# Joining the feed-forward, the second cross attention and the LoRA layer of a gated two-block transformer in one program of eight slots per tile

## The reference

```python
x = x + tanh(g_xattn[0]) * L0_xattn(layernorm(x), ctx, ctx, mask, wq, wk, wv, wo)   # 32 query heads, 8 kv heads, RoPE
x = x + tanh(g_ffn[0])   * L0_ffn(layernorm(x), Wg, Wu, Wd)
x = x + tanh(g_xattn[1]) * L1_xattn(layernorm(x), ctx, Wq, bq, Wk, bk, Wv, bv)
x = x + tanh(g_ffn[1])   * L1_ffn(layernorm(x), W_base, b_base, lora_A, lora_B, router_W, router_b, prior, active)

def L0_ffn(x):            # F = 1376; weights quantised to 4 bits per row, activations to 8 bits per token
    h = silu(quant_linear(x, Wg)) * quant_linear(x, Wu)
    return quant_linear(h, Wd)
def L1_xattn(x, init):    # per sequence: channels C = 64, "time" T = 512
    q, k = Wq @ init + bq, Wk @ init + bk
    return softmax(q.T @ k) @ (Wv @ x + bv)        # T x T weights for each of 16 sequences
def L1_ffn(x):            # four active experts of rank 8
    y = x @ W_base.T + b_base
    alpha = softmax(log(prior + EPS) + router(x))[active]
    return y + sum_e alpha_e * 2.0 * (x @ A_e.T) @ B_e.T
```

## Time and profile before

| | us |
|---|---|
| median of 3 runs (lowest, highest) | 946.81 (945.67, 949.27) |
| the profiled execution, its own time | 948.28 |
| its span, from first to last instruction | 946.3 |

### The profile page before, as it was taken

One profiled execution on the slowest core, in us unless ns is written; L12 is line 12 of the kernel. 1 busy time (PEld: TensorE's weight loads), 2 busy tenths in 40 slices (PEclk: granted clock), 3 DMA queues, 4 the chain that ended last, 5 costly groups with the idle time before them and its releaser, 6 DMA issues. The chain is left out here.

```text
span 946.3 us, 14460 instructions
## 1 busy us (share of the span) xinstructions
PE 856.0 (90%) x5009; PEld 652.6 (69%) x5009; DVE 594.7 (63%) x1291; ACT 485.4 (51%) x1059; POOL 489.1 (52%) x502
## 2 busy tenths in 40 slices
PE   4689999999999999999999999976995688888885
PEld 4567888888888787888888888753442466666664
DVE  3447667676676566665755555677983666666652
ACT  2444556555555454545445434336874666666541
POOL 1477556565575665656656755413454344444441
PEclk9799999999999999999999999988998899999998
DMA  8501221331331330421310405520000000000000
GB/s 239 141 19 56 92 81 35 114 94 34 118 92 29 98 99 11 119 68 29 115 43 18 24 1 204 131 89 1 1 0 1 1 1 12 11 11 11 11 12 23
DMA packets 66796, 54.14 MB, mean 57 GB/s; under 512 B 34560, under 2 KB 52192, under 8 KB 66352
## 3 DMA queue, kind: packets, MB, share of 16 engines
q1 hardware_dynamic: 66448, 53.36, 20.0%
q10 hardware_dynamic: 288, 0.00, 0.0%
HBM read 47.01 MB, written 6.34 MB: 56 GB/s over the span
## 5 line engine op out<-in xcount | busy, mean ns | idle before, releaser
L846 POOL TENSOR_TENSOR rope_swap<-rope_swap,trig 128x512 f32<-128x512 f32 x80 | 108.6, 1357 | 198.4 <-ACT rope_swap L562 197.2
L704 DVE TENSOR_TENSOR rope_cos<-bank,trig 128x512 f32<-128x512 f32 x80 | 55.3, 691 | 135.6 <-PE bank L79 135.6
L561 ACT COPY rope_swap<-bank 64x512 f32<-64x512 f32 x80 | 46.7, 584 | 166.8 <-DVE rope_cos L704 166.8
L1848 POOL TENSOR_TENSOR b_e<-b_e,b_inv 128x512 f32<-128x512 f32 x64 | 66.7, 1041 | 108.0 <-DVE b_inv L1637 108.0
L77 PE MATMUL bank<-xnT_hi,wq_hi 128*128 128x512 f32 x256 | 106.1, 414 | 4.8 <-issue 3.2
L453 PE MATMUL bank<-wo_hi,oT_hi 128*128 128x512 f32 x256 | 106.7, 417 | 1.1 <-ACT oT_hi L639 1.1
L79 PE MATMUL bank<-xnT_hi,wq_lo 128*128 128x512 f32 x256 | 101.5, 396 | 0.0
L78 PE MATMUL bank<-xnT_lo,wq_hi 128*128 128x512 f32 x256 | 101.3, 396 | 0.0
L454 PE MATMUL bank<-wo_lo,oT_hi 128*128 128x512 f32 x256 | 100.8, 394 | 0.0
L731 DVE SCALAR_TENSOR_TENSOR x_res<-bank,gate,x_res 128x512 f32<-128x512 f32 x128 | 88.6, 732 | 3.6 <-PE bank L458 3.6
L852 POOL TENSOR_TENSOR q_rope<-rope_cos,rope_swap 128x512 f32<-128x512 f32 x64 | 84.2, 1315 | 5.0
(11 more groups left out here) (215 smaller groups left out, 2058.9 us busy)
## 6 DMA issues: line engine op xcount, KB each, us to landing
wq_raw<-in_L_xattn_wq SPq DMA_DIRECT2D x16, 512.0 KB, 5.2
wo_raw<-in_L_xattn_wo SPq DMA_DIRECT2D x16, 512.0 KB, 5.5
w_T_dram<-w_out SPq DMA_DIRECT2D x28, 128.0 KB, 3.0
w_T<-w_T_dram SPq DMA_DIRECT2D x2, 1376.0 KB, 7.3
q_rope<-in_ctx SPq DMA_DIRECT2D x4, 512.0 KB, 5.9
wkv_raw<-in_L_xattn_wk SPq DMA_DIRECT2D x8, 256.0 KB, 3.1
wkv_raw<-in_L_xattn_wv SPq DMA_DIRECT2D x8, 256.0 KB, 3.6
x_res<-in_x SPq DMA_DIRECT2D x4, 512.0 KB, 10.0
```

Source lines behind the costliest of these rows:

```text
L704: dve.tensor_tensor(out=rope_cos[:, rp, :].rearrange("p (b s) -> p b s", s=S), in0=proj[pos % 2][:, :].rearrange("p (b s) -> p b s", s=S), ...
L846: pool.tensor_tensor(out=sw, in0=sw, in1=sin_b, op=ALU.mult).then_inc(s_rope, 1)
L1848: pool.tensor_tensor(out=e[n % 4][:, :], in0=e[n % 4][:, :], in1=inv_total[:, n:n + 1].to_broadcast([P, D]), op=ALU.mult).then_inc(s_w, 1)
```

## The change

The first attention stays, but its last three slots on VectorE also take the layer-norm statistics of the first six tiles, which `block1_weights` did before, and after the last slot come their aggregation and one power on GpSimd.

The three later programs become one, `tail_block`. It has 10 iterations of eight slots, all written out. In iteration `it` it works on four tiles: f = it (feed-forward), a = it - 1 (second attention, middle part), y = it - 2 (LoRA layer), nx = it + 1 (q and k of the next tile, and its activation scale). One block of weights runs per slot, m = 8 it + s - 4. The making of the weights is spread over slots 0 to 3 of iteration 0. Further:

- The PSUM banks are shared. `eT_ps` has one bank. `misc_ps` serves q, k, v, the transposes of x, x3 and the end of h. `gate_ps` serves gate, the transpose of h and down. `up_ps` serves up and the first half of the base product with the low-rank columns (292 columns); `y1_ps` the second half and LoRA.
- The weights of q and k stand side by side, so one product makes q and k of one sequence. ScalarE makes the high part of all 128 partitions in one instruction, VectorE the low part in one, and SP copies the halves into the stacked layout with five DMAs per sequence (64 x 512 float32, 128 KB each).
- Silu becomes Tanh: VectorE scales up by half the scale, GpSimd makes gate * up, and VectorE makes (tanh + 1) times that (`make_h`).
- The normalisations of all three layer norms go from VectorE to GpSimd.
- The result is made in three instructions of 256 columns instead of one of 512.

```diff
 def attention_block(...):            # VectorE, slot()
+                if last and jp == 1 and u > 0:
+                    for tl in range(2):
+                        dve.wait_ge(s_acc, 2 * U + tl + 1)
+                        dve.bn_stats(K.stats[:, 2 * u - 2 + tl, :], K.x[:, 2 * u - 2 + tl, :]).then_inc(s_x_stat, 1)
...
-def ffn_block(cx, K, W): ...
-def block1_weights(cx, K, W, R, ctx_dram): ...
-def block1(cx, K, W, out_dram): ...
+def tail_block(cx, K, W, W1, R, ctx_dram, out_dram):
+        def run_slots(slot):
+            for it in range(NT + 2):
+                for s in range(NS):
+                    slot(it, s, NS * it + s - 4, it, it - 1, it - 2, it + 1)
+        # TensorE
+            def gate_up(t, n):
+                if n == 0:
+                    pe.wait_ge(s_xT_sb, t + 1)
+                    after(pe, s_out, t)
+                    after(pe, s_res, t - 2)
...
+            def attend(t, tb):
+                pe.wait_ge(s_eT_sb, NB * t + 2 * tb + 2)
+                if tb == 0:
+                    pe.wait_ge(s_v, t + 1)
...
+            def z_T(t):
+                pe.wait_ge(s_z, 5 * t + 5)
...
+            def slot(it, s, m, f, a, y, nx):
+                if is_logit(m): logits(m)
+                if is_logit(m - 2): weights_T(m - 2)
+                if s == 0: gate_up(f, 0)
+                if s == 1: x3_T(y); gate_up(f, 1)
+                if s == 2: gate_up(f, 2); v_item(a)
+                if s in (3, 4, 5, 6): attend(a, s - 3)
+                if s == 3: base_low(y)
+                if s == 4: qk(nx, 0)
+                if s == 5: z_T(y); qk(nx, 1)
+                if s == 6: h_transpose(f); lora_base(y)
+                if s == 7: down(f); x_transpose(nx)
+        # VectorE (in iteration 0 the steps of the weights stand in slots 0 to 3 as well)
+            def slot(it, s, m, f, a, y, nx):
+                row_max(m)
+                if s == 0: output(a)
+                if s == 1: statistics(a)
+                reciprocal(m)
+                if s == 0: scale_gate_up(f, 0)
+                if s == 1: x3_lo(y); scale_gate_up(f, 1); make_h(f, 0)
+                if s == 2: scale_gate_up(f, 2); make_h(f, 1)
+                if s == 3: make_h(f, 2); add_v(a)
+                if s == 4: route(y); h_scales(f); lo_qk(nx, 0)
+                if s == 5: route_end(y); lo_qk(nx, 1)
+                if s == 6: zT_lo(y); front(nx)
+                if s == 7: finish(y); residual(a)
+        # ScalarE
+            def slot(it, s, m, f, a, y, nx):
+                if s == 7: hT_copy(f)
+                if s == 5: h_int(f)
+                copy_T(m - 2); exps(m)
+                if s == 0: tanh_half(f, 0)
+                if s == 1: x3_hi(y); tanh_half(f, 1)
+                if s == 2: tanh_half(f, 2)
+                if s == 4: route_exp(y); h_shifted(f); hi_qk(nx, 0)
+                if s == 5: hi_qk(nx, 1); zT_copy(y)
+                if s == 6: x_shifted(nx); x_int(nx)
+                if s == 7: xT_copy(nx)
+        # GpSimd
+            def slot(it, s, m, f, a, y, nx):
+                weigh(m - 1)
+                if s == 0: add(a)
+                if s in (1, 2, 3): product(f, s - 1)
+                if s == 1: std(a); normalise(a)
+                if s == 5: add_bias(y); front(nx)
+                if s == 7: x3_std(a); x3_normalise(a)
+        # SyncE
+            def duplicate(t, par):
+                after(sp, s_r, NB * (t - 1))
+                sp.wait_ge(s_qk_lo, 2 * t + par + 1)
+                for dst, src in ((q_stack[i][par][lower, :], qk_hi[par][lower, :]), ...):   # five
+                    sp.dma_start(f32(dst), f32(src)).then_inc(s_dup[i][par], 16)
+            # slot 5: duplicate(nx, 0); slot 6: duplicate(nx, 1), the next context tile; slot 7: store(y)
```

More of the change, by code:

```diff
@@ new lines, in tail_block @@
+        e = [sb(f"b_e{i}", [P, D]) for i in range(4)]
+        eT = sb2("b_eT", [P, DC, D])
+        bT = e[0]
+        x3_stats, x3_mv, x3_ve, x3_rstd = sb("b_x3_stats", [P, 6]), sb("b_x3_mv", [P, 2]), sb("b_x3_ve", [P, 1]), sb("b_x3_rstd", [P, 1])
+        pad = sb("b_pad", [P, 1])
+        logit, neg_lmax, lsum, linv = sb("b_logit", [P, E_ACT]), sb("b_neg_lmax", [P, 1]), sb("b_lsum", [P, 1]), sb("b_linv", [P, 1])
+        alpha = sb("b_alpha", [P, E_ACT])
+        z = sb("b_z", [P, ZREP, E_ACT, RANK])
@@ new lines, in tail_block, with ok, is_logit, after @@
+        s_y, s_res = sem("s_b_y"), sem("s_b_res")
+        s_part = sem("s_b_part")
+        s_store = [sem(f"s_b_store{i}") for i in range(2)]
+        def run_slots(slot):
+            for it in range(NT + 2):
+                for s in range(NS):
+                    slot(it, s, NS * it + s - 4, it, it - 1, it - 2, it + 1)
+        def ok(t):
+            return 0 <= t < NT
+        def is_logit(m):
+            return 0 <= m < NB * NT
+        def after(eng, s, value):
+            if value > 0:
+                eng.wait_ge(s, value)
@@ new lines, in _ @@
+            front(0)
+            selection()
+            def slot(it, s, m, f, a, y, nx):
+                if is_logit(m):
+                    row_max(m)
+                if s == 0:
+                    if ok(a):
+                        output(a)
+                if s == 1 and ok(a):
+                    statistics(a)
+                if is_logit(m):
+                    reciprocal(m)
+                if s == 0:
+                    if it == 0:
+                        base_lo(0)
+                        lo_qk(0, 0)
+                    if ok(f):
+                        scale_gate_up(f, 0)
+                if s == 1:
+                    if it == 0:
+                        base_lo(1)
+                        lo_qk(0, 1)
+                    if ok(y):
+                        x3_lo(y)
+                    if ok(f):
+                        scale_gate_up(f, 1)
+                        make_h(f, 0)
+                if s == 2:
+                    if it == 0:
+                        base_lo(2)
+                        base_lo(3)
+                    if ok(f):
+                        scale_gate_up(f, 2)
+                        make_h(f, 1)
+                if s == 3:
+                    if it == 0:
+                        low_lo()
+                        low_b_lo()
+                        rest_of_weights()
+                        late_statistics()
+                    if ok(f):
+                        make_h(f, 2)
+                    if ok(a):
+                        add_v(a)
+                if s == 4:
+                    if ok(y):
+                        route(y)
+                    if ok(f):
+                        h_scales(f)
+                    if ok(nx):
+                        lo_qk(nx, 0)
+                if s == 5:
+                    if ok(y):
+                        route_end(y)
+                    if ok(nx):
+                        lo_qk(nx, 1)
+                if s == 6:
+                    if ok(y):
+                        zT_lo(y)
+                    if ok(nx):
+                        front(nx)
+                if s == 7:
+                    if ok(y):
+                        finish(y)
+                    if ok(a):
+                        residual(a)
```

1513 lines of the change are left out of this document (694 added, 819 removed).

## The result

The changed kernel takes 1041.95 us (median of 4 runs, 1041.03 to 1042.75) against 946.28 us (945.67 to 949.27) for the kernel before in the same session: a ratio of 1.1004, 95% interval 1.0978 to 1.1029. It is slower, as forecast, and inside the range of 965 to 1048, but 29 us above the forecast of 1013 and above the 998 to 1028 that the forecast gave as its own range. The profiled execution has a span of 1040.4 us at a mean granted clock of 0.924 (before: 946.3 and 0.968).

A forecast was written before the change was run, and what follows sets the result against it. The second attention was taken as paced by VectorE's own list, waits included. List and exponential waits 29.0 + stalls 11.3 + clock 2.4 + make_h 1.0 gave P = 43.7; 706.3 + 7 P = 1012.2, forecast 1013 us, range 965 to 1048.

The forecast's parts named there:

- slots 3 and 4, b_v to the logits: VectorE's maximum in slot 4 waits for attend, twelve products and logits queued behind b_v: 3.5 us.
- clock: After TensorE's two long waits per iteration, 3 us each at the lower clock: 2.4 us, bounds 0 and 5.
- neighbouring iterations 42 to 45 us apart: Sign in the new trace: the same VectorE step in neighbouring iterations stands 42 to 45 us apart.
- the upper end, three full lengths: Three make_h per tile, each blocked by GpSimd for up to its full length: 3 us; 1.0 was taken.
- the price put on that (1.5 per tile): Normalisation on GpSimd, bounded by 0.53 and 2.1 us: costs 0 at the 1.04 taken, 1.5 per tile at the upper end.
- 706.3 + 7 P: Whole span from the tail's start, edge iterations and P, the period of one iteration: 1012.2 us at P = 43.7.
- iteration 8: 20; iteration 9: 17.2: The last two tail iterations: 20 us, then 17.2 us for the LoRA chain alone at half clock and the store.
- The break-even: The iteration period at which the changed kernel equals the kernel before: P = 34.3 us.
- Rival B: Run-ahead leaves VectorE only its list and six unfilled exponentials: P = 29.0, 905 us; chance 0.12.
- A: Rival: TensorE keeps its full clock and make_h is not blocked: P = 40.3, 989 us; chance 0.22.
- D: Rival: the DMA copies are late, more than 6 us each: P some 52, 1071 us; chance 0.03.
- C: Rival: make_h blocking at its upper end, GpSimd normalisations at 2.1 us, low clock after each wait: 1045 us; chance 0.15.

The follow-up runs named there:

- e_fill: Changed kernel plus unread TensorE products (12 before the first attend, 18 before the transpose of z) during its waits: 1022.32 us.
- e_norm: Changed kernel with a tile's three normalisations moved back from GpSimd to VectorE: 1045.13 us.
- e_b2: e_b1 with VectorE steps already due placed between maximum and reciprocal in slots 2, 4, 6 and 7: 939.01 us, ratio 0.9898.
- e_b1: Changed kernel with the reorderings of e_addv, e_low, e_qk, h_int behind the exponential, lora_base in slot 7, residual before finish: 971.02 us.
- e_b3: e_b2 with b_v before slot 2's make_h, last make_h and route_end filling exponential waits, slot 5's high q and k before h_int: 913.76 us.
- e_late: Changed kernel with a tile's ten DMA copies issued only after down of the tile before: 1041.20 us.
- e_addv: Changed kernel with VectorE's b_v step in slot 3 moved between the maximum and the reciprocal: 1022.72 us.
- e_low: Changed kernel with TensorE's twelve 292-column products moved in slot 3 ahead of the first attend: 1023.02 us.
- e_rec: Changed kernel with VectorE steps already due placed between maximum and reciprocal in slots 2, 4, 6 and 7: 1002.90 us.
- e_qk: Changed kernel with slot 4's high half of q and k before h_shifted, and slot 5's second q and k before the transpose of z: 1029.19 us.
- e_hint: Changed kernel with ScalarE's h_int (slot 5) and copies of transposed h (slot 7) moved behind the slot's exponential: 1044.65 us.

## Why the prediction was right, and where its size was off

The forecast rested on VectorE's list per iteration and on stalls named one by one. Against the timeline of one iteration (809.77 to 856.42, 46.65 us):

| step | predicted | measured | at full clock (e_fill) |
|---|---|---|---|
| VectorE's list, with make_h blocked | 25.2 | 25.43 | 25.43 |
| waits for exponentials, slots 2 to 7 | 6.1 | 6.48 | 6.49 |
| slot 0, gate behind output | 1.1 | 1.10 | 1.10 |
| slots 3 and 4, b_v to the logits | 3.5 | 5.84 | 3.51 |
| slot 4, first lo_qk | 2.1 | 1.85 | 1.85 |
| slot 5, second lo_qk | 2.1 | 3.00 | 2.00 |
| slots 6 and 7, logits behind lora_base | 1.5 | 1.34 | 1.33 |
| waits for GpSimd (x_res, the product) | none | 1.00 | 1.00 |
| clock | 2.4 | in the rows above, 3.3 | 0 |

(Overlap was put at -0.3; gaps of VectorE too short for the view are 0.6.)

- The mechanism was right in every place it named, and e_fill gives each row back to within 0.4 us once the clock is held up. But the sign named for it, neighbouring iterations 42 to 45 us apart, was missed: they stand 45.9 to 47.2 apart. The walk through the order, with durations from the trace of before, was enough to find them.
- The clock was undersized: "2.4 us" was 3.3 by the two stalls (2.9 by P in e_fill). The prediction took 3 us at the lower level after each wait, and it was six after the first (0.50 from 872 to 878): attend, products and logits all ran in it.
- `make_h` was sized rightly: 24 of them take 21.6 us; at 0.68, 0.68 and 0.52 unblocked they would be 15.0, so 0.8 us per tile against the 1.0 taken. The instance at 868.28 takes 1.43 us and ends 0.55 after the `weigh` that began at 868.12 ended. The Trainium skill (SBUF — State Buffer, Who interferes with whom) says that the one that comes second is blocked for all of the other; this row agrees. Another does not: the first `make_h` of the tile starts 0.36 us into a GpSimd normalisation of 2.08 us and takes 0.95, where the rule would hold it beyond 865.91.

```profile
863.83 2.08 POOL L1760 TENSOR_SCALAR b_xn<-x_res,b_meanvar,b_rstd 128x512 f32<-128x512 f32 x1
```

```profile
864.19 0.95 DVE L1351 SCALAR_TENSOR_TENSOR f_h<-f_tanh,f_up 128x512 f32<-128x512 f32 x1
```

  So the upper end, three full lengths, did not come about: one of the three meets a `weigh` ahead of it, one this normalisation, and the third (0.53 at 871.25) starts before the `weigh` beside it.
- GpSimd's operation took 2.08 us, the upper bound; the price put on that (1.5 per tile) was too dear, since it delays only `b_xn` by 0.9 us in TensorE's list, and b_v waits for make_h in any case. e_norm, which takes the step off GpSimd and gains nothing, bears this out.
- Left out: two waits for GpSimd, 1.0 us per iteration. With 0.9 for the clock, the 0.6 of small gaps and the 0.3 of overlap that did not come, they are most of the 2.9 us by which this iteration is longer than 43.7.
- The span was to be 706.3 + 7 P = 1012.2; it is 1040.4. Of the 28.2 us, the five whole iterations hold 13.8 (2.75 each), iteration 7 4.1, the last two 9.7 and all before them 0.6. The term that was furthest off for its size is the edge "iteration 8: 20; iteration 9: 17.2": the last two took 46.9 us at a granted clock of 0.66. In e_b2, in its other order, they take 37.0 at 0.82, near the 37.2 of the prediction; how much of the 9.7 us is clock and how much waiting no run separates.
- The break-even was put at P = 34.3. On a line between e_b1 (36.58, 971.0) and e_b2 (31.46, 939.0), the 948 us of before lie at P = 32.9.
- Rival B was wrong for the changed kernel. Its P = 29.0 is what e_b3 reaches (28.84), not by run-ahead but by another order, in which the exponentials of slots 2 to 7 are nearly filled and other short waits are left; that the two numbers meet is luck. A was out by the clock, D by e_late. C's 1045 us was the nearest of the times given, for a wrong sum: GpSimd's 2.1 us were there and cost nothing.

## What to carry to other kernels

Joining programs wins only what the written order lets engines overlap: here the join as ordered cost 10%, and the same instructions in another order gain 3.7%. Walk each engine's list for a step that another engine waits for right behind it, put independent work there (TensorE's products before the attend, VectorE's steps inside the wait for an exponential), and test exchanges together too: some pay alone (e_addv, e_low, e_rec), others hand half of their gain (e_qk) or all of it (e_hint) to the next wait. The long waits of TensorE here (4.4 and 5.8 us) cost their length and then the lower clock that follows, 2.9 us per iteration.
